# Sums over partitions moved from GpSimd to TensorE, and the first block's unfold copied inside SBUF

## The chip, the cores and the metric

The kernel runs on one core of one Trainium2 chip. The metric is device time in microseconds (us) for one execution, as the median of several runs. A smaller number is better. The page and the trace come from one profiled execution, which has its own time and its own span.

The engines are called as in the trace: PE is TensorE, DVE is VectorE, ACT is ScalarE, POOL is GpSimd, SP is SyncE, which here only issues transfers. SPq, ACTq, DVEq and POOLq are the sequencers of these engines, and PEld is the loading of weights into PE.

## What is computed

The input is x of 16 batches, each 128 rows by 1024 columns, with a context of the same shape. The block does two gated steps:

```
xn  = layernorm(x)
sim = cosine similarity of each ctx column with its left neighbour, itself, its right neighbour
att_out[o,t] = sum over (c,k) of weight[o,c,k] * xn[c, t+k-1] * sim[k,t]     (K = 3)
x1  = x + tanh(g_xattn) * att_out

h   = relu(layernorm(x1) @ up_w) ** 2            (1024 -> 2048)
s   = h @ down_w                                  (2048 -> 1024)
r   = ((layernorm(x1) @ fc1_w) @ expert_w) * routing_sum @ fc2_w
out = x1 + tanh(g_ffn) * layernorm(s + r)
```

The routing sum of a row is the sum of the two largest of eight logits, layernorm(x1) @ gate_w.

The unfold is the step that matters here: the 128 x 3 = 384 rows (channel c, shift k) of shifted xn, in the order 3c + k, are laid over three groups of 128 partitions, so that PE can contract over them. Row r of the unfolded matrix is channel r // 3, shifted by r % 3.

Matmuls of the steady part run on pairs of float16 numbers, a high and a low part. Each weight is first scaled by a power of two. The exponent comes from a sum or a maximum over the whole weight, so it needs a reduction over the 128 partitions. There are five such scales besides up_w's: the two small weights w_xattn and w_gate (WX, WG, computed together), fc1 (WF1), the product expert x fc2 (W2E) and down_w (WDN).

## The kernel before, in words

The 16 batches are taken in NB = 4 blocks of BB = 4 batches, j = 0 to 3. For each block there is an attention step (called phase a), then `up_half` (20 tiles t of the latent and hidden layer, 24 matmuls each), then `down_half` (for each batch 96 matmuls of `shared` and 24 of `routed`). The attention step of block m + 1 is woven into `up_half(m)` and `down_half(m)`. The attention step of block 0 has nothing to be woven into: it stands alone at the front with the loading, scaling and splitting of all weights. This front is where the change lies.

Each engine runs its own written list of instructions in order. The engines meet at semaphores. Nothing is reordered at run time, so what stands behind a waiting instruction on an engine waits too. SP's list issues nearly all loads and stores, and holds a wait wherever a transfer needs a buffer or data.

Names, in the order of the front:

- ACT's `first_f_pairs(j)` normalises batch j and writes the high part (semaphore f_hi). POOL subtracts to make the low part (line 575, f_rdy). ACT's batch j >= 2 waits until POOL is done with batch j - 2. The pair lies in `fp[j]`.
- DVE takes the maxima of each partition of the two small weights into `amx` (amax_rdy 1). POOL reduces these over the partitions with `partition_all_reduce` (line 579), which stands in POOL's list between the low part of batch 0 and that of batch 1 (amax_all 1). The same is done for fc1 (line 582), for W2E (line 601) and for down_w (line 607, inside `up_half(0)`).
- ACT's square root at line 848 stands behind all four `first_f_pairs`. DVE's `first_cosines` needs it (line 999 on), and only then can SP store the similarities and load them back, spread over 128 partitions (`first_sims(j)`, lines 338 and 339).
- SP's `first_unfold(j)` waits for f_rdy, writes the pair three times to DRAM with shifts of 0, 1 and 2 columns (line 322, 512 KB each), waits for these to land, and reads the unfolded rows back in one transfer of 1.5 MB (line 333) into `U[j % 2]` (u_buf for even j, a part of lgb for odd j).
- SP's order behind that is: unfold(0), load of fc1, store of the similarities, sims(0), unfold(1), sims(1), unfold(2), sims(2), three loads of up_w (line 481), unfold(3), sims(3), five more loads of up_w. unfold(2) and unfold(3) wait for PE to have used the buffer (p_done).
- PE's `xattn(0, j, h)` (line 1363) uses `U`, for each half h of the columns. DVE's `combine(0, j)` (lines 1043 to 1059) applies the similarities and adds, ACT's line 677 normalises, PE turns (line 1384).
- ACT's `up_squares(k)` (line 814) squares a 1 MB slice of up_w when it has landed, and PE sums the squares by columns (line 1522). They stand between the batches' steps in ACT's list. After them come DVE's scale of up_w (line 1293 and behind), W2E's scale, and the splitting of 16 tiles of up_w (ACT line 769, DVE line 1163), with which `up_half(0)` begins.

## Time and profile before

| what | us |
|---|---|
| median of 3 runs | 1131.89 |
| lowest and highest of them | 1130.33, 1138.74 |
| the profiled execution: its time | 1136.75 |
| the profiled execution: its span | 1135.0 |
| PE busy in the span | 1005.7 (89%) |
| DVE busy | 553.9 (49%) |
| ACT busy | 301.0 (27%) |
| POOL busy | 256.0 (23%) |
| moved by transfers | 175.31 MB |

The busy share of an engine is an average over the whole span. The page's second part cuts the span in 40 slices of 28.4 us: PE shows 5, 5, 8, 5, 6 tenths in the first five, the front, and 9 nearly everywhere from slice 13 on. The transfer engines show 8, 4, 9, 8, 7 tenths in the first five and 2 to 5 tenths for most of the rest.

In a row of the timeline the first number is the start from the span's start, the second the time from there to the end of the last of the group. What stands in square brackets is how long the engine had been idle, and what ended it. "issue" there means that the engine waited for nothing that the profile shows.

### The profile page before, as it was taken

How to read it: one execution, taken by the hardware profiler on the slowest of the kernel's cores; microseconds unless marked ns; L12 is line 12 of the kernel's file. 1: busy time of each engine (PE TensorE's matmuls, PEld its weight loads, DVE VectorE, ACT ScalarE, POOL GpSimd, SP SyncE). 2: the span in 40 equal slices, each digit the busy share in tenths (PEclk: the TensorE clock that was granted, in tenths of full speed). 3: DMA queues.
4: the chain of work that ended last, by engine and by line, in shares of the span. 5: the costliest groups of instructions: out<-in, count | busy, mean ns of one | idle time of the engine just before them, and what ended most of it. 6: DMA issues, size and time to landing. Idle time of an engine off the chain costs nothing.

```text
span 1135.0 us, 13061 instructions
## 1 busy us (share of the span) xinstructions
PE 1005.7 (89%) x4773; PEld 466.4 (41%) x4775; DVE 553.9 (49%) x987; ACT 301.0 (27%) x413; POOL 256.0 (23%) x170
## 2 busy tenths in 40 slices
PE   5585699486779999999899999997999999999996
PEld 4232243132334444444344444443444444444442
DVE  3367677457674552666354553674455522221112
ACT  4335554564311111223011121232011112220110
POOL 4211112227452223222022113330022220000121
PEclk9698699787889999999899999999999999999998
DMA  8498788843533323374433325556233323310000
GB/s 296 165 308 325 289 296 292 322 179 111 188 129 130 129 94 133 115 263 173 137 130 111 112 94 187 202 201 226 93 130 104 105 89 107 99 38 1 19 19 38
DMA packets 55587, 175.31 MB, mean 154 GB/s; under 512 B 6818, under 2 KB 7010, under 8 KB 54498
## 3 DMA queue, kind: packets, MB, share of 16 engines
q1 hardware_dynamic: 50050, 155.05, 39.0%
q10 hardware_dynamic: 5472, 19.40, 4.5%
q8 instruction: 40, 0.66, 0.3%
q14 instruction: 25, 0.20, 0.1%
HBM read 130.26 MB, written 44.17 MB: 154 GB/s over the span
## 4 chain that ended last, share of the span: by engine, by line
PE 61%; DMA 11%; DVE 8%; issue 8%; POOL 3%; ACT 3%; DVEq 2%; SPq 1%; POOLq 1%; ACTq 1%
PE psS L1426 27%; PE psS L1399 12%; PE psR L1399 10%; PE psR L1437 7%; PE psP L1363 5%; DMA shift_scratch<-hid 4%; DMA work<-in_x 2%; DMA u_buf<-shift_scratch 1%; DMA scr<-in_ctx 1%; DMA pair_scratch<-hid 1%; POOL f_pair L521 1%; POOLq L503 1%; DMA big<-in_L_ffn_up_w 1%; DMA shift_scratch<-f_pair 1%; DVE hid L1163 1%
## 5 line engine op out<-in xcount | busy, mean ns | idle before, releaser
L1426 PE MATMUL psS<-big,hid 128*128 128x512 f16 x1536 | 346.3, 385 | 7.9 <-ACT y L699 7.9
L1399 PE MATMUL psS<-xT,ring 128*128 128x512 f16 x960 | 216.3, 386 | 18.7 <-DMA ring<-pair_scratch 14.8
L1426 PEld LDWEIGHTS psS<-big,hid 128*128 128x128 f16 x1536 | 151.5, 99 | 192.3 <-issue 10.0
L1399 PE MATMUL psR<-xT,ring 128*128 128x512 f16 x960 | 214.2, 383 | 9.6 <-DMA ring<-pair_scratch 8.2
L1399 PEld LDWEIGHTS psS<-xT,ring 128*128 128x128 f16 x960 | 94.8, 99 | 136.6 <-DMA ring<-pair_scratch 15.2
L1399 PEld LDWEIGHTS psR<-xT,ring 128*128 128x128 f16 x960 | 94.0, 98 | 126.7 <-issue 10.2
L513 POOL TENSOR_TENSOR y<-y,lgb 128x1024 f32<-128x1024 f32 x15 | 35.2, 2346 | 490.6 <-ACT y L691 490.6
L647 ACT ACTIVATE sd<-sd 128x1 f32<-128x1 f32 x44 | 8.9, 202 | 374.5 <-DVE sd L917 374.5
L1437 PE MATMUL psR<-w,lgb 128*128 128x512 f16 x384 | 86.0, 379 | 0.0
L1363 PE MATMUL psP<-u_buf,wx 128*128 128x512 f16 x252 | 62.8, 397 | 11.3 <-DMA u_buf<-shift_scratch 8.8
L1200 DVE TENSOR_TENSOR hid<-sim_side,hid 128x512 f16<-128x512 f32 x64 | 53.1, 829 | 34.9 <-ACT hid L726 32.9
L1125 DVE SCALAR_TENSOR_TENSOR y<-psR,rw,y 128x1024 f32<-128x1024 f32 x15 | 19.2, 1282 | 102.3 <-PE psR L1437 99.9
L1043 DVE SCALAR_TENSOR_TENSOR scr<-psP,coef,sim_side 128x512 f32<-128x512 f32 x28 | 20.9, 748 | 97.0 <-PE psP L1363 89.9
L726 ACT ACTIVATE hid<-sim_side 128x512 f16<-128x512 f32 x64 | 40.3, 630 | 95.9 <-DVEq L1194 95.9
L1437 PEld LDWEIGHTS psR<-w,lgb 128*128 128x128 f16 x384 | 37.5, 98 | 44.7
L501 POOL TENSOR_TENSOR sides<-scr 128x1023 f32<-128x1023 f32 x12 | 22.7, 1890 | 121.3 <-DMA scr<-in_ctx 104.3
L1191 DVE SCALAR_TENSOR_TENSOR sim_side<-psS,sim_side 128x512 f32<-128x512 f32 x32 | 22.1, 690 | 50.6 <-ACT sim_side L724 49.8
L908 DVE BATCH_NORM_STATS2 st<-work 128x6 f32<-128x512 f32 x52 | 34.8, 688 | 19.1 <-DMA work<-in_x 16.9
L1363 PEld LDWEIGHTS psP<-u_buf,wx 128*128 128x128 f16 x252 | 24.9, 101 | 45.5 <-issue 16.4
L1191 DVE SCALAR_TENSOR_TENSOR sim_side<-psR,sim_side 128x512 f32<-128x512 f32 x32 | 22.0, 689 | 40.0 <-ACT sim_side L724 38.8
L521 POOL TENSOR_TENSOR f_pair<-work,f_pair 128x1024 f16<-128x1024 f32 x12 | 26.0, 2164 | 56.5 <-ACT f_pair L671 56.5
L1106 DVE TENSOR_TENSOR xT<-psP,xT 128x512 f16<-128x512 f32 x25 | 16.1, 686 | 41.5 <-ACT xT L684 41.5
(225 smaller groups left out, 1002.4 us busy)
## 6 DMA issues: line engine op xcount, KB each, us to landing
ring<-pair_scratch SPq DMA_DIRECT2D x80, 512.0 KB, 5.8
u_buf<-shift_scratch SPq DMA_DIRECT2D x14, 1536.0 KB, 6.4
shift_scratch<-f_pair SPq DMA_DIRECT2D x39, 512.0 KB, 3.8
work<-in_x SPq DMA_DIRECT2D x26, 512.0 KB, 5.8
big<-in_L_ffn_up_w SPq DMA_DIRECT2D x8, 1024.0 KB, 14.1
pair_scratch<-hid ACTq DMA_DIRECT2D x16, 512.0 KB, 5.6
out_rows<-y SPq DMA_DIRECT2D x15, 512.0 KB, 2.6
sim_side<-side_scratch SPq DMA_DIRECT2D x14, 512.5 KB, 4.1
```

The lines of the kernel that those rows point to most:

```text
L501: pool.tensor_tensor(sides_a[:, 0:T - 1], scr[0][:, 0:T - 1], scr[0][:, 1:T], ALU.mult)
L513: pool.tensor_tensor(y[:, :], y[:, :], gam, ALU.mult)
L521: pool.tensor_tensor(fp[0][:, 1, 1:T + 1], work[:, 0, :], fp[0][:, 0, 1:T + 1], ALU.subtract)\
L726: act.activation(hT[:, t - LT, 0, :], buf, ACT.Copy).then_inc(h_hi, 1)
L908: dve.bn_stats(st[:, k, h, :], src[:, HALF * h:HALF * h + HALF])
L1043: dve.scalar_tensor_tensor(out=left, in0=psP[:, 0, :], scalar=c_x, in1=sim_side[b][:, t0:t0 + HALF], op0=ALU.mult, op1=ALU.mult)
L1191: dve.scalar_tensor_tensor(out=hbuf[:, t % 2, :], in0=bank, scalar=0.0, in1=hbuf[:, t % 2, :], op0=ALU.max, op1=ALU.mult)
L1200: dve.tensor_tensor(hT[:, t - LT, 1, :], hbuf[:, t % 2, :], hT[:, t - LT, 0, :], ALU.subtract).then_inc(h_rdy, 1)
L1363: mm = pe.matmul(psP[:, g, :], wx[:, g, w, :], U[b][:, g, v, t0:t0 + HALF], start=(n == 0), stop=(n == 2))
L1399: mm = pe.matmul(up_bank[t % NR], ring[:, t % NR, a, k, :], xT[:, k, b, :], start=(k == 0 and a == 0 and b == 0), stop=(k == KB - 1 and a ...
L1426: mm = pe.matmul(psS[:, HALF * h:HALF * h + HALF], hT[:, i, a, P * j:P * j + P], dn[:, i, b, HALF * h:HALF * h + HALF], start=(i == 0 and ...
L1437: mm = pe.matmul(psR[:, HALF * h:HALF * h + HALF], lat[:, l, a, P * j:P * j + P], w2[:, l, b, HALF * h:HALF * h + HALF], start=(l == 0 and ...
```

## The change

Five edits belong together.

1. The four `partition_all_reduce` of POOL are taken out. In their place PE multiplies a 128 x 128 matrix of ones (`ones_f`, one more memset on POOL) with the one or two columns of `amx`, so that each partition of a PSUM column holds the sum (`norm_over_rows`). DVE copies that column into `amr` before it computes the power of two. For WX and WG the maximum over partitions becomes a sum of the partitions' maxima.
2. These matmuls have fixed places in PE's list: WX and WG behind `first_sums`; WF1 between `xattn(0, 0, 0)` and `expert_fc2(1)`; W2E ahead of `up_half(0)`; WDN behind tile t = 12 of `up_half(0)`. Each waits for `amax_rdy`.
3. `first_unfold(j)` no longer goes through DRAM. It copies from `fp[j]` to `U[j % 2]` inside SBUF. For each of the three groups and three shifts one transfer of 42 rows (168 KB, to every third partition) is issued, and for six of the nine one more transfer of a single row: 15 transfers for a batch, 60 for the block, where there had been four, 16 for the block. There is no wait between them any more.
4. Counts of semaphores that follow from it: `u_in` counts 15 transfers for a batch of the first block, `shift_out` starts from zero with block 1, and ACT's `f_pairs` of the first batch of block 1 does not wait for it.
5. `combine(0, j)` on DVE first waits for f_rdy of a batch two ahead (it overwrites the buffer `scr` that POOL reads), and ACT drains behind the square of fc1.

```diff
+    ROWS = P // G
+    UIN_0 = 16 * (G * G + P * G - ROWS * G * G)
...
+        norm_at = {WX: psP[:, 2, 8:10], WF1: psM[:, 500:501], W2E: psP[:, 2, 0:1], WDN: psP[:, 2, 1:2]}
...
@@ SP, first_unfold(j)
                 sp.wait_ge(f_rdy, j + 1)
                 sp.wait_ge(pads_rdy, 1)
                 if j >= 2:
-                    sp.wait_ge(u_in[j % 2], UIN * (j // 2))
-                shifts_out(j, j)
-                sp.wait_ge(shift_out, 16 * G * (j + 1))
-                if j >= 2:
                     sp.wait_ge(p_done, 2 * (j - 1))
                 if j == 1:
                     sp.wait_ge(eT_done, LT)
-                unfold_into(j, j % 2)
+                for g in range(G):
+                    for k in range(G):
+                        p0 = (k - P * g) % G
+                        c0 = (P * g + p0) // G
+                        num = (P - p0 + G - 1) // G
+                        p1 = p0 + G * ROWS
+                        sp.dma_start(U[j % 2][p0:p1 - G + 1:G, g, :, :],
+                                     fp[j][c0:c0 + ROWS, :, k:k + T]).then_inc(u_in[j % 2], 16)
+                        if num > ROWS:
+                            sp.dma_start(U[j % 2][p1:p1 + 1, g, :, :],
+                                         fp[j][c0 + ROWS:c0 + ROWS + 1, :, k:k + T]).then_inc(u_in[j % 2], 16)
@@ POOL
+            pool.memset(ones_f[:, :], 1.0)
...
-                if j == 0:
-                    pool.wait_ge(amax_rdy, 1)
-                    pool.partition_all_reduce(amr[:, WX:WG + 1], amx[:, WX:WG + 1], P, RMAX)\
-                        .then_inc(amax_all, 1)
-            pool.wait_ge(amax_rdy, 2)
-            pool.partition_all_reduce(amr[:, WF1:WF1 + 1], amx[:, WF1:WF1 + 1], P, RADD).then_inc(amax_all, 1)
...
-            pool.wait_ge(amax_rdy, 3)
-            pool.partition_all_reduce(amr[:, W2E:W2E + 1], amx[:, W2E:W2E + 1], P, RADD).then_inc(amax_all, 1)
...
-                    if first and j == BB - 1:
-                        pool.wait_ge(amax_rdy, 4)
-                        pool.partition_all_reduce(amr[:, WDN:WDN + 1], amx[:, WDN:WDN + 1], P, RADD)\
-                            .then_inc(amax_all, 1)
@@ DVE, combine and norm_scale
                 if first:
+                    dve.wait_ge(f_rdy, min(j + 3, BB))
                     dve.wait_ge(sim_in[b], 32 * (j // 2 + 1))
...
                 dve.wait_ge(amax_all, turn)
+                dve.tensor_copy(amr[:, k:k + 1], norm_at[k])
+                dve.drain()
@@ PE
+            def norm_over_rows(k, n, turn):
+
+                pe.wait_ge(amax_rdy, turn)
+                pe.matmul(norm_at[k], ones_f[:, :], amx[:, k:k + n], start=True, stop=True,
+                          skip_group_check=True).then_inc(amax_all, 1)
...
                     mm.then_inc(up_done, 1)
+                    if first and t == SCALE_T:
+                        norm_over_rows(WDN, 1, 4)
...
             pe.drain().then_inc(sums_done, 1)
+            norm_over_rows(WX, 2, 1)
...
             xattn(0, 0, 0)
+            norm_over_rows(WF1, 1, 2)
             expert_fc2(1)
...
             pe.wait_ge(norms_read, 1)
-            up_half(0, True)
+            pe.wait_ge(comb, 2 * BB)
+            norm_over_rows(W2E, 1, 3)
+            up_half(0, True, True)
```

SP's list before, from the unfold of batch 0 to the reading back of batch 1 (f_pair and hid hold the pairs, u_buf and lgb the unfolded rows):

```order
L322 DMA shift_scratch<-f_pair 128x2x1024 [waits pads_rdy,f_rdy]
L322 DMA shift_scratch<-f_pair 128x2x1024 x2
L333 DMA u_buf<-shift_scratch 128x3x2048 [waits shift_out]
L468 DMA big<-in_L_ffn_fc_w 128x8x512
L314 DMA side_scratch<-hid 32x128 [waits simo_rdy]
```

The same stretch of SP's list now:

```order
L383 DMA u_buf<-f_pair 42x2x1024 [waits pads_rdy,f_rdy]
L386 DMA u_buf<-f_pair 1x2x1024
L383 DMA u_buf<-f_pair 42x2x1024
L386 DMA u_buf<-f_pair 1x2x1024
L383 DMA u_buf<-f_pair 42x2x1024 x2
L386 DMA u_buf<-f_pair 1x2x1024
...
L477 DMA big<-in_L_ffn_fc_w 128x8x512
L317 DMA side_scratch<-hid 32x128 [waits simo_rdy]
```

The wait on shift_out is gone from between the two halves of the unfold, and 15 issues stand where four stood.

PE's list now, in `up_half(0)` around tile t = 12; the fourth row is new, the others stood there before in this order:

```order
L1409 MATMUL psR<-xT,ring 128x512 x23
L1409 MATMUL psS<-xT,ring 128x512 [waits up_evac,ring_in0]
L1409 MATMUL psS<-xT,ring 128x512 x23
L1329 MATMUL psP<-amx,ones_f 128x1 [waits amax_rdy]
L1409 MATMUL psS<-xT,ring 128x512 [waits up_evac,ring_in1]
L1409 MATMUL psS<-xT,ring 128x512 x23
```

Tile 13 and all behind it now stand behind a wait for amax_rdy, which on PE there was not.

## Rows read from the trace of the kernel before

**Rows 1.** Busy us by stage; columns: stretch, length, engines, PEclk, DMA share, GB/s
```profile
0.00:142.30 142.30, 88.00 (x347) 47.30 (x349) 77.36 (x140) 61.44 (x67) 35.70 (x52) 0.83 0.77 277
142.30:295.50 153.20, 115.93 (x548) 51.34 (x549) 100.67 (x135) 79.45 (x109) 50.15 (x32) 0.87 0.65 235
...
668.00:910.00 242.00, 231.72 (x1134) 106.71 (x1133) 126.08 (x239) 49.96 (x78) 52.31 (x28) 0.99 0.43 148
```

**Rows 2.** Chain of waits in the front: start us, us, what
```profile
68.39 17.28 DMA shift_scratch<-hid
...
89.60 17.50 DMA shift_scratch<-hid
...
108.53 11.02 DMA big<-in_L_ffn_up_w
```

**Rows 3.** Timeline of POOL, 20 to 66 us: start, us, instruction, idle before
```profile
30.74 0.37 POOL L579 PARTITION_ALL_REDUCE amr<-amx  x1 [5.83 <-issue]
40.82 2.13 POOL L575 TENSOR_TENSOR hid<-hid 128x1024 f16<-128x1024 f32 x1 [9.71 <-issue]
```

**Rows 4.** Timelines of ACT, DVE and PE, 40 to 66 us
```profile
43.06 1.24 ACT L660 ACTIVATE hid<-hid,rs_x 128x1024 f32<-128x1024 f32 x1 [13.81 <-POOL hid L575]
45.66 2.06 DVE L999 TENSOR_SCALAR hid<-hid 32x129 f32<-32x129 f32 x1 [12.47 <-ACT hid L848]
47.59 9.80 PE L1510 MATMUL psS<-big,home 128*128 128x512 f32 x16 [11.25 <-ACT home L852]
61.96 0.75 DVE L1043 SCALAR_TENSOR_TENSOR scr<-psP,coef,sim_side 128x512 f32<-128x512 f32 x1 [7.07 <-DMA ring<-self_scratch]
```

**Rows 5.** Timeline of SP: issues of the unfold and of up_w
```profile
24.94 2.67 SPq L322 DMA_DIRECT2D shift_scratch<-f_pair  x3
31.18 0.36 SPq L333 DMA_DIRECT2D u_buf<-shift_scratch  x1
...
87.10 1.41 SPq L481 DMA_DIRECT2D big<-in_L_ffn_up_w  x3
...
108.53 2.48 SPq L481 DMA_DIRECT2D big<-in_L_ffn_up_w  x5
```

**Rows 6.** Timelines of ACT and PE, 72 to 125 us
```profile
82.02 4.02 PE L1363 MATMUL psP<-lgb,wx 128*128 128x512 f16 x9
83.80 1.02 ACT L821 ACTIVATE w<-psS 128x1024 f32<-128x1024 f32 x1 [2.83 <-DMA pair_scratch<-xT]
113.47 4.02 PE L1363 MATMUL psP<-lgb,wx 128*128 128x512 f16 x9 [9.17 <-DMA lgb<-shift_scratch]
119.58 1.91 ACT L814 ACTIVATE sides<-big 128x2048 bf16<-128x2048 f32 x1 [11.34 <-DMA big<-in_L_ffn_up_w]
```

**Rows 7.** Timelines of POOL and DVE where W2E's scale is made
```profile
145.26 0.40 POOL L601 PARTITION_ALL_REDUCE amr<-amx  x1 [5.88 <-issue]
145.69 0.15 DVE L1111 TENSOR_SCALAR amr<-amr 128x1 f32<-128x1 f32 x1 [3.50 <-POOL amr L601]
```

**Rows 8.** Timelines of four engines where down_w's scale is made
```profile
242.34 0.40 POOL L607 PARTITION_ALL_REDUCE amr<-amx  x1 [6.46 <-DVEq L1169]
252.59 1.88 POOL L501 TENSOR_TENSOR sides<-scr 128x1023 f32<-128x1023 f32 x1 [9.84 <-issue]
251.51 0.57 ACT L724 ACTIVATE sim_side<-psS 128x512 f32<-128x512 f32 x1
254.59 1.25 DVE L951 STREAM_TRANSPOSE y<-sides 128x1024 f32<-128x1024 f32 x1 [1.79 <-POOLq L503]
245.05 8.26 PE L1399 MATMUL psR<-xT,ring 128*128 128x512 f16 x24 [3.75 <-DMA ring<-pair_scratch]
```

**Rows 9.** Rates and small instructions: transfers at 86 to 108 us, matmul, copy
```profile
86.00:108.00 22.00, 14.99 (x54) 7.02 (x54) 19.51 (x31) 14.13 (x17) 5.08 (x4) 0.97 0.89 334
...
268.88 0.57 PE L1327 MATMUL psM<-fold,part 128*128 128x1 f32 x2
...
299.72 0.18 DVE L1136 COPY lg<-psM 128x32 f32<-128x32 f32 x1
```

More of the change, by code:

```diff
@@ L25 @@
 I32 = mybir.dt.int32
-RMAX = bass.bass_isa.ReduceOp.max
-RADD = bass.bass_isa.ReduceOp.add
 P = 128
@@ L138, in flamingo_block @@
         ones_b = sb("ones_b", [P, P], BF16)
+        ones_f = sb("ones_f", [P, P], F32)
         pick = sb("pick", [P, 2 * BB * KB - 1], F32)
@@ L341, in first_unfolded @@
             def first_unfolded(m):
-                sp.wait_ge(shift_out, ahead(16 * G * BB * (m + 1)))
+                sp.wait_ge(shift_out, ahead(16 * G * BB * m))
                 unfold_into(0, 0)
@@ L667, in f_pairs @@
                 act.wait_ge(rs_rdy[LX], q + 1)
-                act.wait_ge(shift_out, 16 * G * q)
+                if not (isinstance(q, int) and q == BB):
+                    act.wait_ge(shift_out, 16 * G * (q - BB))
                 act.activation(work[:, 0, :], work[:, 0, :], ACT.Identity, bias=rs[:, LX, 1:2], scale=rs[:, LX, 0:1])
@@ L812, in up_squares @@
                 elif n == 1:
-                    act.wait_ge(u_in[0], UIN)
+                    act.wait_ge(u_in[0], UIN_0)
                 act.activation(squares[n % 2], up_raw[:, k, :], ACT.Square).then_inc(sq_rdy, 1)
@@ L860, in _ @@
             act.wait_ge(f1_in, 16)
-            act.activation(fc1_junk, fc1_raw, ACT.Square, accum_out=amx[:, WF1:WF1 + 1]).then_inc(amax_rdy, 1)
+            act.activation(fc1_junk, fc1_raw, ACT.Square, accum_out=amx[:, WF1:WF1 + 1])
+            act.drain().then_inc(amax_rdy, 1)
             w2_evac(0)
@@ L892, in _ @@
             for b in range(2):
-                act.wait_ge(u_in[b], 2 * UIN)
+                act.wait_ge(u_in[b], 2 * UIN_0)
             act.wait_ge(home_rdy, BB)
@@ L1271, in _ @@
             dve.wait_ge(amax_all, 1)
+            dve.tensor_copy(amr[:, WX:WG + 1], norm_at[WX])
+            dve.drain()
             pow2(WX, WG + 1, amr[:, WX:WG + 1], 2.0 ** -23, 0.0)
@@ L1285, in _ @@
                 .then_inc(gate_w_rdy, 1)
-            dve.wait_ge(amax_all, 2)
-            pow2(WF1, WF1 + 1, amr[:, WF1:WF1 + 1], 2.0 ** -24, 63.5)
+            norm_scale(WF1, 2)
             dve.drain().then_inc(scale_rdy, 1)
@@ L1350, in xattn @@
                 elif first:
-                    pe.wait_ge(u_in[b], UIN * (j // 2 + 1))
+                    pe.wait_ge(u_in[b], UIN_0 * (j // 2 + 1))
                     if j == 0:
@@ L1357, in xattn @@
                 else:
-                    pe.wait_ge(u_in[0], UIN * (q - 1))
+                    pe.wait_ge(u_in[0], 2 * UIN_0 + UIN * (q - BB + 1))
                     pe.wait_ge(xt_rdy, 2 * q)
@@ L1386, in turn_first, with up_half @@
                 mm.then_inc(tr_done, 1)
-            def up_half(n, phase_a):
+            def up_half(n, phase_a, first=False):
                 m = n + 1
```

## The prediction, made before the changed kernel had run

> **What bounds the kernel now.** I read the busy time by stage first, then the chain of waits, then the timelines of the front. The stages [rows 1] show that PE works 231.72 of 242.00 us in an ordinary block: there it is the bound, and the change touches nothing there. In the front it works 88.00 of 142.30 us, and in the first `up_half` 115.93 of 153.20. From the first `down_half` on the program is the same instructions in the same order, so what the front loses or gains should reach the end one to one. The question is only when the front's last results are there.
>
> Two things stretch the front. The first is POOL. It finished the low part of batch 0 at 24.9, and then stood 5.83 us before the first all-reduce ran and 9.71 us behind it before it could make the low part of batch 1 [rows 3]. ACT waited 13.81 us for that low part, and with it the square root that stands behind; DVE waited 12.47 us for the square root, and PE 11.25 us for ACT's copies of the expert weights behind the same list [rows 4]. The second is SP's queue. The chain of waits runs through the landing of the shifted copies in DRAM, 17.28 us for batch 2 and 17.50 us for batch 3, and only then are the last five loads of up_w issued, at 108.53; the first of these lands 11.02 us later [rows 2]. ACT had been idle 11.34 us for it, and PE 9.17 us for the unfolded rows of batch 3 [rows 6]. The transfers were busy 77% of the front at 277 GB/s [rows 1], which is much, but not all.
>
> **The change, part by part.**
>
> POOL without the first all-reduce. ACT was free at 43.06 - 13.81 = 29.2 and had made the high parts of batches 1 and 2 just before, 2.3 us each, so that of batch 1 was ready about 27, before the first all-reduce had begun to run. Its low part then takes 2.13 us [rows 3] and ends at 29, when ACT is just free. So ACT's 13.81 us go entirely. DVE's square root comes then at about 32.4 instead of 45.6; DVE itself reaches line 999 about a microsecond sooner too, since WX's result comes from a small matmul as soon as `first_sums` has ended. What stays of the 12.47 us is under half a microsecond. PE's 11.25 us go the same way. The three inputs of the first `combine` (PE's product, the similarities, and their transfer, for which DVE waited 7.07 us until 61.96 [rows 4]) all hang on this one root and move together: I take **13.0 us**, with ends at 12.0 and 13.8. The all-reduce of WF1 had other work beside it (PE's fc2 product) and is costed at nothing; if that cover went, 6 us would show, but the product is 9.80 us long [rows 4].
>
> Here a page bears on the size. The trace shows a gap of 5.83, 5.88 and 6.46 us ahead of three all-reduces and of 9.71 and 9.84 us behind two of them [rows 3, 7, 8]. The Trainium skill, GPSIMD Engine Reference, section "Instruction dispatch", states about 6 us for the first call to a freshly loaded kernel; of the way back to ordinary instructions it says nothing. By the page alone this term would be near 6 us instead of 13. The trace has the gap behind as well, both times.
>
> The middle of the front. The wait of ACT for the stored fc1 pairs, 2.83 us [rows 6], stood behind 1.5 MB of shifted copies in the same queue; a queue with half that traffic should shorten it. Ends 0 and 2.83; **2 us**.
>
> The unfold inside SBUF. For each batch three writes, a wait and one read become 15 copies. The issue of a transfer costs SP 0.89 us by the three at 24.94, 0.47 by the three at 87.10 and 0.50 by the five at 108.53 [rows 5]; the first row holds the one that the engine had just been waiting for, so I take 0.47, and 15 copies cost 7 us, at most 13. Nothing else of SP's is late by that: up to batch 1, the load of fc1 goes out behind the 15 copies at about 24.9 + 7 = 32, where it was 31.6. For batches 2 and 3 the wait for the landing is gone and the wait for PE's use of the buffer remains. For batch 3 that is the second half of batch 1, which ended at 86.0 [rows 6]. Moved by 13 + 2 it ends at 71; 7 us of copies and 1 us for the similarities bring the five loads of up_w to 79, where they were at 108.53. With the same 11.02 us to land [rows 2] the first is there at 90. ACT was ready for it at 119.58 - 11.34 = 108.2, which becomes 93. So the wait falls to nothing with 3 us to spare. PE's 9.17 us lie beside ACT's and are no term of their own.
>
> The bytes speak the same: each batch now moves 1.5 MB instead of 3. From the unfold of batch 1 on, about 14 MB have to pass before ACT's slice is there (three unfolds 4.7, three pairs of similarities 3.1, stored fc1 2.1, four slices of up_w 4.2), and at the 334 GB/s of a loaded stretch [rows 9] that is 42 us, from 43, when the first of them is issued, to 85. So the gain is the full 11.34 if the copies run at the rate of other transfers, and nothing if they run so slowly that they bring the old wait back. I take **10 us**; ends 0 and 11.34.
>
> W2E. DVE waited 3.50 us for the all-reduce [rows 7]. In its place stand a matmul of one column, about 0.3 us (two took 0.57 [rows 9]), a copy of 0.18 [rows 9] and a drain: 0.8 in all with the semaphores. **2.7 us**; ends 2.0 and 3.2.
>
> WDN. DVE reached its result late, and it was not waited for. But POOL, 9.84 us behind it, came late with the products that DVE waited 1.79 us for [rows 8]; that can come back. Against it, PE now waits behind tile 12 for amax_rdy, which DVE posted just before POOL's 242.34 [rows 8]. Tile 13 starts then at 242.5 instead of right behind tile 12. With the granted clock down after such a pause a tile of 24 takes up to 8.26 us [rows 8], so tile 13 is there by 250.8; ACT took it at 251.51 [rows 8]. The cover is thus 0.7 us at its thinnest: PE was two tiles ahead of ACT there, its tile 15 ended at 253.3 [rows 8], and this lead is what gets used up. Ends -3 and +1.79; I take **0**.
>
> The new copies on DVE, ACT's drain and the memset are 0.2 us each; they are in the terms above or beside idle time. DVE's added wait for f_rdy of a batch two ahead is met at about 34, before the first `combine`.
>
> Sum: 13.0 + 2 + 10 + 2.7 + 0 = 27.7 us. The profiled execution took 1136.75, so 1109.0 by it. The median of the runs shown is 1131.89, which is 4.9 lower, so the forecast is **1104 us**.
>
> **The rivals.**
>
> The copies bring the wait for up_w back. Copies with 42 rows and an odd shift could run well below the 334 GB/s, and the transfers are the fullest resource of the front. Then the third term is lost: 27.7 - 11 gives 17, or 1115. For it: 77% busy already. 
>
> Slower: the copies are served one after another, each with its own fixed time d. Three unfolds lie on the front's path, 45 copies. The forecast has 21 us in them and 3 to spare; all 27.7 are eaten when 45 d = 21 + 3 + 27.7, so d = 1.15 us. At 1.3 us it is 7 us slower, 1139. Against it: three shifted copies of 512 KB were issued in 2.67 us and had all landed by 31.18 [rows 5], 2.1 us a piece with three times the bytes, and 172 KB at 334 GB/s are 0.5 us. The same page, section "Rules for kernel authors", calls transfers under 64 KB mostly overhead and counsels to merge them. By its fixed 2 us for a transfer, taken one after another, the copies would make the kernel 1170. Chance 5%, and 8% for the stretch between, within 1% of before.
>
> **How the numbers follow.** The forecast holds 61%, with its own range 1097 to 1111: ends of the terms add to about 33 at best, and the two ends of 0 and -3 seldom come together. The range 1096 to 1118 takes in most of the first rival too. A measurement of this kernel can tell about 1% from no change, 11.3 us, so faster is below 1120.6. That is the forecast, the second rival and nearly all of the first: 0.87. Within 1%: 0.08. Slower: 0.05.
>
> **What would show each step.** POOL's low part of batch 1 starts near 27 and ACT's idle before line 660's last row is gone. DVE reaches the first `combine` near 49. SP issues 15 copies in about 7 us and the last five loads of up_w near 79. ACT doesn't wait for up_w, and DVE's scale of up_w comes some 25 us sooner. W2E costs DVE under 1 us. PE has a gap of 12 us behind tile 12 without a later tile of ACT moving. From then on every row is 28 us earlier. It is wrong if SP is seen issuing a copy in over 1 us, or if the unfolded rows land over 10 us behind the last issue.

## The result, and the profile after

The changed kernel took 1118.38 us (median of 4 runs, 1116.14 to 1118.85) beside 1131.71 us for the kernel before on the same chip (4 runs). The ratio is 0.9861, with a 95% interval of 0.9833 to 0.9889. The forecast was 1104 us, with a range of 1096 to 1118. The sign was right. The size was about half to two thirds of what was forecast: as it stands the median lies 0.4 us above the range, and by its ratio, on the 1131.89 us that the forecast started from, it is 1116.2, just inside. The profiled execution took 1118.56 us, with a span of 1116.7, which is 18.3 us shorter than the one before (1135.0), where 27.7 were forecast. The medians are only 13.3 us apart, since the profiled execution of the kernel before (1136.75 us) was itself 5 us above its median. The steps below are differences of these two executions; a repeat (experiment 5) gave 19.4 us between medians.

The stages come first. Columns: stretch, length, busy us of PE, PEld, DVE, ACT and POOL, granted clock, DMA share, GB/s.

```profile
0.00:142.30 142.30, 98.90 (x405) 51.38 (x408) 86.56 (x157) 68.51 (x73) 40.10 (x54) 0.89 0.76 258
142.30:295.50 153.20, 122.94 (x581) 55.05 (x580) 98.61 (x139) 79.94 (x109) 55.57 (x33) 0.88 0.64 232
668.00:910.00 242.00, 231.80 (x1135) 106.88 (x1134) 126.14 (x239) 50.24 (x77) 52.04 (x29) 0.99 0.41 147
```

Against [rows 1], an ordinary block is the same (231.80 us of PE beside 231.72), and the two front stages hold 10.9 and 7.0 us more of PE's work: work has moved forward. The first matmul of the first `down_half` tells how far (timeline of PE, the kernel before and then the changed one; columns: start us, us, instruction).

```profile
295.55 14.67 PE L1426 MATMUL psS<-big,hid 128*128 128x512 f16 x60
```

```profile
276.82 14.89 PE L1438 MATMUL psS<-big,hid 128*128 128x512 f16 x60
```

It is 18.7 us earlier, and that accounts for the gain of the span (18.3). The rest of this section follows it back.

**The start of the front.** Timelines of POOL, DVE and PE of the changed kernel. The bracket is the idle time ahead of an instruction and what ended it.

```profile
27.02 2.15 POOL L585 TENSOR_TENSOR hid<-hid 128x1024 f16<-128x1024 f32 x1 [2.15 <-ACT hid L660]
33.52 0.44 DVE L999 TENSOR_SCALAR hid<-hid 32x129 f32<-32x129 f32 x1 [0.40 <-ACT hid L847]
35.67 7.13 PE L1523 MATMUL psS<-big,home 128*128 128x512 f32 x16 [0.84 <-ACT home L851]
49.90 0.59 PE L1329 MATMUL psM<-amx,ones_f 128*128 128x1 f32 x2 [5.15 <-ACTq L861]
52.19 0.75 DVE L1044 SCALAR_TENSOR_TENSOR scr<-psP,coef,sim_side 128x512 f32<-128x512 f32 x1 [0.76 <-DMA ring<-self_scratch]
```

POOL's low part of batch 1 starts at 27.02 where it started at 40.82 [rows 3], and of the four waits of 12.47, 11.25, 13.81 and 9.71 us [rows 3, 4] less than 1 us is left on any engine, besides POOL's 2.15 us for ACT. DVE is at line 999 at 33.52 instead of 45.66, 12.1 us earlier. But its first `combine` is at 52.19 instead of 61.96 [rows 4], only 9.8 earlier. Two arrivals that stand ahead of it were late, and within a microsecond of each other. One is WF1's scale, which DVE computes just ahead of `combine`: PE waited 5.15 us before the one-column sum for it. The other came last, by 0.76 us: the similarities, read back from DRAM. SP's timeline of the changed kernel, and then of the kernel before, where the store had gone out at 53.09:

```profile
39.34 0.36 SPq L317 DMA_DIRECT2D side_scratch<-hid  x1
46.47 0.36 SPq L341 DMA_DIRECT2D sim_side<-side_scratch  x1
```

```profile
54.98 0.36 SPq L338 DMA_DIRECT2D sim_side<-side_scratch  x1
```

The store was 13.75 us earlier, but the load that has to wait for it to land came 7.1 us behind it, where it had been 1.9. It went out just after fc1 had landed (46.11, below). Both late arrivals thus lead to the load of fc1.

**SP's queue.** Timeline of SP, with the 42-row copies (L383) and single rows (L386) of batches 0 and 2, and the loads behind them. "x3" joins three issues.

```profile
24.90 1.04 SPq L383 DMA_DIRECT2D u_buf<-f_pair  x1
...
36.48 0.63 SPq L386 DMA_DIRECT2D u_buf<-f_pair  x1
37.16 0.40 SPq L477 DMA_DIRECT2D big<-in_L_ffn_fc_w  x1
...
61.89 0.88 SPq L383 DMA_DIRECT2D u_buf<-hid  x1
...
68.91 1.78 SPq L386 DMA_DIRECT2D u_buf<-hid  x1
...
76.74 0.63 SPq L386 DMA_DIRECT2D u_buf<-hid  x1
...
78.76 1.66 SPq L490 DMA_DIRECT2D big<-in_L_ffn_up_w  x3
80.54 0.88 SPq L383 DMA_DIRECT2D lgb<-hid  x1
...
94.53 0.63 SPq L386 DMA_DIRECT2D lgb<-hid  x1
```

And the same issues by line; columns: instructions, then shortest, median and longest ns of one.

```profile
L383 SPq DMA_DIRECT2D u_buf<-f_pair x9: 807/852/1043, 24.9 to 35.6; - x9
L386 SPq DMA_DIRECT2D u_buf<-f_pair x6: 616/635/649, 26.0 to 36.5; - x6
L383 SPq DMA_DIRECT2D u_buf<-hid x9: 807/871/2237, 61.9 to 75.8; - x9
```

A 42-row copy costs SP 0.85 us and a single row 0.64, where 0.47 was assumed. The 15 of batch 0 take 37.11 - 24.90 = 12.2 us and those of batch 1 take 12.0; those of batches 2 and 3 take 15.5 and 14.6, as some single issues stretch to 1.8 and more there, with the transfers busy (0.88 from 60 to 96 us, shown with the seventh experiment). From 61.89 until the last five loads of up_w go out, SP issues almost without a pause.

**The end of the front.** Timelines of ACT, PE and DVE, changed kernel.

```profile
46.11 3.62 ACT L860 ACTIVATE home<-big 128x4096 bf16<-128x4096 f32 x1 [9.79 <-DMA big<-in_L_ffn_fc_w]
73.23 1.02 ACT L820 ACTIVATE w<-psS 128x1024 f32<-128x1024 f32 x1 [1.98 <-DMA pair_scratch<-xT]
97.95 4.02 PE L1373 MATMUL psP<-lgb,wx 128*128 128x512 f16 x9 [5.21 <-DMA lgb<-hid]
105.65 1.91 ACT L813 ACTIVATE sides<-big 128x2048 bf16<-128x2048 f32 x1 [8.98 <-DMA big<-in_L_ffn_up_w]
129.03 0.16 DVE L1175 COPY amr<-psP 128x1 f32<-128x1 f32 x1 [0.77 <-PE psP L1329]
129.28 0.15 DVE L1112 TENSOR_SCALAR amr<-amr 128x1 f32<-128x1 f32 x1
223.23 0.59 PE L1329 MATMUL psP<-amx,ones_f 128*128 128x1 f32 x2 [11.28 <-DVEq L1170]
```

SP issues the last five loads of up_w at 96.53 (shown with the third experiment), and ACT's wait for them is still 8.98 us, where it was 11.34 [rows 6]. ACT is there at 105.65 instead of 119.58, 13.9 earlier. The first instruction of W2E's scale, at 129.28 behind the new copy, is 16.4 earlier than the same one at 145.69 [rows 7], so 2.5 came from its all-reduce. PE's stand of 11.28 us behind tile 12 was foreseen. The start of `down_half` is 2.3 us further ahead than W2E was, so no cost of the stand shows here; the eighth experiment prices it.

### The profile page after: what moved, and what is told of

Same layout as the page of the kernel before. It is cut to its first block, busy times and chain, and to the rows that moved or that the text cites. A ratio compares the mean times of both kernels' runs of the same rounds, so it can differ in the third digit from the quotient of the medians.

```text
span 1116.7 us, 13108 instructions
## 1 busy us (share of the span) xinstructions
PE 1004.0 (90%) x4781; PEld 466.2 (42%) x4783; DVE 550.6 (49%) x991; ACT 301.2 (27%) x413; POOL 256.2 (23%) x167
## 4 chain that ended last, share of the span: by engine, by line
PE 64%; issue 9%; DMA 7%; DVE 7%; SPq 4%; POOL 3%; ACT 3%; DVEq 2%; POOLq 1%; ACTq 0%
PE psS L1438 28%; PE psS L1409 12%; PE psR L1409 10%; PE psR L1449 7%; PE psP L1373 5%; SPq L383 2%; DMA pair_scratch<-hid 2%; DMA u_buf<-shift_scratch 1%; SPq L386 1%; POOL f_pair L530 1%; DMA scr<-in_ctx 1%; DMA shift_scratch<-f_pair 1%; POOL scr L513 1%; PE psR L1523 1%; DMA big<-in_L_ffn_up_w 1%
## 5 line engine op out<-in xcount | busy, mean ns | idle before, releaser
L1409 PE MATMUL psS<-xT,ring 128*128 128x512 f16 x960 | 221.1, 392 | 12.5 <-DMA ring<-pair_scratch 10.9
L1409 PE MATMUL psR<-xT,ring 128*128 128x512 f16 x960 | 210.8, 379 | 3.7 <-DMA ring<-pair_scratch 3.7
L1409 PEld LDWEIGHTS psS<-xT,ring 128*128 128x128 f16 x960 | 96.4, 101 | 133.2 <-issue 15.4
L1126 DVE SCALAR_TENSOR_TENSOR y<-psR,rw,y 128x1024 f32<-128x1024 f32 x15 | 19.2, 1282 | 102.3 <-PE psR L1449 99.8
L1203 DVE TENSOR_TENSOR hid<-sim_side,hid 128x512 f16<-128x512 f32 x64 | 49.3, 770 | 34.9 <-ACT hid L725 32.9
L725 ACT ACTIVATE hid<-sim_side 128x512 f16<-128x512 f32 x64 | 40.3, 630 | 94.5 <-DVEq L1197 94.5
```

Of the source, the lines that this page charges most:

```text
L725: act.activation(hT[:, t - LT, 0, :], buf, ACT.Copy).then_inc(h_hi, 1)
L1203: dve.tensor_tensor(hT[:, t - LT, 1, :], hbuf[:, t % 2, :], hT[:, t - LT, 0, :], ALU.subtract).then_inc(h_rdy, 1)
L1409: mm = pe.matmul(up_bank[t % NR], ring[:, t % NR, a, k, :], xT[:, k, b, :], start=(k == 0 and a == 0 and b == 0), stop=(k == KB - 1 and a ...
```

## The experiments

The question was where the rest had gone. **Theory S**: SP's time for the issues. 15 copies hold its queue for 12 us or more, so that the load of fc1 and those of up_w go out late. **Theory T**: the transfer engines are nearly full, and the loads of up_w would land late whenever they were issued. The names behind the headings are those that the expectations use. The before-kernel's median was 1135.68 us beside the first four experiments, 1137.43 beside the next four and 1133.58 beside the last two; ratios go by these.

**1. The sums on TensorE alone.** (e1_sums_only) The unfold goes through DRAM as before.

```diff
-                for g in range(G):
-                    for k in range(G):
...
+                shifts_out(j, j)
+                sp.wait_ge(shift_out, 16 * G * (j + 1))
...
+                unfold_into(j, j % 2)
```

> The sums and maxima are on PE as in the changed kernel, the first block's unfold goes through DRAM as before. Theory S (SP's issue time: in the changed kernel a 42-row copy took SP 0.85 us and a single row 0.64 us, 12.2 us for the 15 of a batch, so the unfold inside SBUF gave away most of what it saved): the POOL stall is the main gain, 12.5 to 13 us at the first combine, plus 2.7 at W2E and up to 2 at WDN, and the old unfold keeps its waits; 1113 to 1118 us, level with the changed kernel or a few us better. Rival T (the transfers' bytes bound the front, and the unfold inside SBUF with half of them is a gain of its own): 1121 to 1125, slower than the changed kernel by 3 us or more.

Measured: 1121.5 us, ratio 0.9881 (0.9858 to 0.9903), so 14 us of gain (11 to 16). DVE, SP's queue and ACT, in the profile of this kernel:

```profile
51.34 0.75 DVE L1037 SCALAR_TENSOR_TENSOR scr<-psP,coef,sim_side 128x512 f32<-128x512 f32 x1 [2.04 <-DMA ring<-self_scratch]
98.38 2.52 SPq L484 DMA_DIRECT2D big<-in_L_ffn_up_w  x5
109.59 1.91 ACT L806 ACTIVATE sides<-big 128x2048 bf16<-128x2048 f32 x1 [11.51 <-DMA big<-in_L_ffn_up_w]
```

ACT's wait for up_w is as long as before (11.51 us), and it ends 10.0 us earlier than the 119.58 of [rows 6]. Most of the whole change's gain is this part. The loads of up_w leave only 1.9 us later than with the copies, although the unfolds of four batches through DRAM stand ahead of them. `down_half` begins at 280.15, 3.3 us later than in the changed kernel: that is what the unfold inside SBUF adds to the sums, against the 10 us forecast for it. The theories are not told apart. On the 1132 us of the expectations, S had meant a gain of 14 to 19 us and T one of 7 to 11, so the gain is at S's lower end and above T's; but T's "3 us or more" behind the changed kernel is what the two traces show, while the intervals of the two ratios overlap.

**2. The unfold inside SBUF alone.** (e2_unfold_only) POOL keeps its all-reduces.

```diff
+                if j == 0:
+                    pool.wait_ge(amax_rdy, 1)
+                    pool.partition_all_reduce(amr[:, WX:WG + 1], amx[:, WX:WG + 1], P, RMAX)\
+                        .then_inc(amax_all, 1)
...
```

> The unfold runs inside SBUF as in the changed kernel, the four reductions stay on POOL. Theory S: POOL's stall hides nothing of the 12 us that SP now needs for each batch, but the waits for landings are gone too; the last five loads of up_w are issued near 99 us instead of 108.5, ACT's wait for them is shorter, and the kernel gains 2 to 8 us on the one before: 1124 to 1130. If all gains were additive as in the prediction it would gain 10 to 12: 1120 to 1122. Rival T: with half the bytes ACT waits no longer for up_w at all: 1120.

Measured: 1126.83 us, ratio 0.9921 (0.9899 to 0.9943), 9 us of gain (6.5 to 11.5). By its median that is just above the 2 to 8 of theory S and below the 10 to 12 of additive gains. The timeline of POOL:

```profile
30.85 0.37 POOL L587 PARTITION_ALL_REDUCE amr<-amx  x1 [5.95 <-issue]
38.10 2.13 POOL L583 TENSOR_TENSOR hid<-hid 128x1024 f16<-128x1024 f32 x1 [6.88 <-issue]
```

POOL's stall is there with both gaps, so it belongs to the all-reduce; the second gap is 6.88 us here and was 9.71. 14 and 9 make 23, and the two together gave 16 to 18 (by 0.9861 here, by 0.9844 in the repeat below). The traces say it more sharply: `down_half` begins 15.4 us earlier with the sums alone, 9.2 with the unfold alone (286.39), and 18.7 with both. So the parts share a resource. That it is SP's queue, which the copies have made fuller, is the reading that experiments 3 and 6 test.

**3. The load of fc1 ahead of the first copies.** (e3_fc1_first) Nothing else is changed.

```diff
-            first_unfold(0)
             sp.dma_start(fc1_raw, w_fc1.rearrange("(k p) l -> p k l", p=P)).then_inc(f1_in, 16)
+            first_unfold(0)
```

> The changed kernel with one edit: SP issues the load of fc1 ahead of the 15 copies of batch 0 instead of behind them. In the changed kernel it went out at 37.2 and landed at 46.1, ACT squared it then, and PE waited 5.15 us for the WF1 sum in front of the second fc2 product. Theory S (SP's issue time shifts fc1, fc1 holds PE's list): the load goes out at 25, lands near 32, PE has no wait at WF1, and the first combine starts near 49 instead of 52.2: 3 us better, 1115. Rival (the first combine is held by the similarities' landing, not by the WF1 sum): under 1 us, 1118.

Measured: 1114.35 us, ratio 0.9808 (0.9783 to 0.9834); the interval overlaps that of the changed kernel's repeat (0.9823 to 0.9866) a little. PE, DVE, SP and ACT:

```profile
47.34 0.28 PE L1329 MATMUL psM<-amx,ones_f 128*128 128x1 f32 x2
48.84 0.75 DVE L1044 SCALAR_TENSOR_TENSOR scr<-psP,coef,sim_side 128x512 f32<-128x512 f32 x1 [0.27 <-issue]
41.23 0.37 SPq L341 DMA_DIRECT2D sim_side<-side_scratch  x1
92.31 3.91 SPq L490 DMA_DIRECT2D big<-in_L_ffn_up_w  x5
101.20 1.91 ACT L813 ACTIVATE sides<-big 128x2048 bf16<-128x2048 f32 x1 [8.71 <-DMA big<-in_L_ffn_up_w]
```

In the changed kernel these loads left later (timeline of SP):

```profile
96.53 3.43 SPq L490 DMA_DIRECT2D big<-in_L_ffn_up_w  x5
```

PE's 5.15 us are gone, the first `combine` is at 48.84 instead of 52.19, and the loads, ACT's scale and the end of the front (272.86 instead of 276.82) are all about 4 us earlier. One transfer behind 15 issues instead of ahead of them had cost 4 us: that agrees with theory S for this place. It does not decide against the rival in the expectation, that the similarities' landing holds `combine`: their load too went out 5.2 us earlier, at 41.23 instead of 46.47, 1.9 us behind its store. Experiment 1 shows that this path would have held alone. There PE waited only 0.40 us for WF1, and yet `combine` stood 2.04 us for the similarities and began at 51.34, 0.85 earlier than in the changed kernel. Both paths had to be freed, and the one edit frees both.

**4. Six of the up_w loads ahead of batch 3's copies.** (e4_upw_early)

```diff
-                for k in (UP_ORDER[0:3], UP_ORDER[3:8])[j - 2]:
+                for k in (UP_ORDER[0:6], UP_ORDER[6:8])[j - 2]:
```

> The changed kernel with one edit: six of the eight loads of up_w are issued ahead of the unfold of batch 3 instead of three. In the changed kernel ACT waited 8.98 us for the fourth. Theory S (the fourth load was late because SP spent 14.7 us on issuing the copies of batch 3 ahead of it): ACT's wait goes, PE's wait for the unfolded rows of batch 3 (5.21 us) stays or grows by 1 to 2; 5 to 8 us better, 1110 to 1113. Rival T (the transfer engines were the limit, so what goes earlier delays the unfold by as much): within 2 us of the changed kernel, 1117 to 1120.

Measured: 1120.16 us, ratio 0.9862 (0.9837 to 0.9887): no gain. The timeline of PE:

```profile
106.48 4.02 PE L1373 MATMUL psP<-lgb,wx 128*128 128x512 f16 x9 [14.24 <-DMA lgb<-hid]
```

ACT no longer waited for up_w, but PE waited 14.24 us for batch 3's rows, instead of 5.21: their last copy was issued at 95.5 and PE could start only at 106.5, 11.0 us later, with 6 MB of weights issued ahead of these copies; in the changed kernel it was 94.5 and 97.95, 3.4 us. So the engines that move the bytes are a second limit. Reordering alone changed who is late, as theory T has it, and S's forecast for this run (1110 to 1113) was wrong.

**5. The changed kernel once more** (e0_after_again), with no edit, as the measure for the next three.

> The changed kernel again, beside the kernel before and the variants on one chip. The ratio to the kernel before should be 0.984 to 0.989. Theory S+T (SP's issue time and the full transfer queues together hold the front) and the prediction's own sum differ here only in that the sum of 27.7 us would give 0.976; the sum is excluded if the interval stays above 0.980.

Measured: 1118.06 us, ratio 0.9844 (0.9823 to 0.9866). The five loads leave at 96.40 and ACT's wait is 9.33 us until 105.50: the same picture. The interval lies above the 0.976 that the forecast's sum of 27.7 us would give.

**6. Each 42-row copy cut into 32 and 10 rows.** (e6_rows_32_and_10) The bytes are the same, with 24 issues for a batch instead of 15. If SP's issues are the limit, the time must grow with their number.

```diff
+                        pm = p0 + G * 32
-                        sp.dma_start(U[j % 2][p0:p1 - G + 1:G, g, :, :],
-                                     fp[j][c0:c0 + ROWS, :, k:k + T]).then_inc(u_in[j % 2], 16)
+                        sp.dma_start(U[j % 2][p0:pm - G + 1:G, g, :, :],
+                                     fp[j][c0:c0 + 32, :, k:k + T]).then_inc(u_in[j % 2], 16)
+                        sp.dma_start(U[j % 2][pm:p1 - G + 1:G, g, :, :],
+                                     fp[j][c0 + 32:c0 + ROWS, :, k:k + T]).then_inc(u_in[j % 2], 16)
```

> The changed kernel with each copy of 42 rows cut into one of 32 rows and one of 10. Question: why does a 42-row copy cost SP 0.85 us and a row 0.64 us, while a copy of 128 rows by 4 KB cost it 0.47? Theory K (SP pays extra where a copy does not spread evenly over the 16 queues: 42 rows and 1 row do not, 32 rows do): a 32-row copy costs 0.4 to 0.5 us, a 10-row copy 0.6 to 0.85. Rival N (the cost follows the number of rows, or the step of three partitions, or SBUF on both sides): a 32-row copy costs 0.75 to 0.8 us, a 10-row copy 0.65 to 0.7. With 24 copies for a batch the issue takes 12 to 14 us by K and 17 us by N; the kernel is 0 to 4 us slower by K, 8 to 14 us by N.

Measured: 1135.1 us, one run; the whole gain is gone. Timelines of SP, ACT and PE (L384 is the 32-row copy, L386 the 10-row one, L389 the single row):

```profile
27.39 0.65 SPq L384 DMA_DIRECT2D u_buf<-f_pair  x1
28.09 0.81 SPq L386 DMA_DIRECT2D u_buf<-f_pair  x1
28.93 0.63 SPq L389 DMA_DIRECT2D u_buf<-f_pair  x1
...
42.90 0.41 SPq L480 DMA_DIRECT2D big<-in_L_ffn_fc_w  x1
...
116.33 2.80 SPq L493 DMA_DIRECT2D big<-in_L_ffn_up_w  x5
124.54 1.91 ACT L816 ACTIVATE sides<-big 128x2048 bf16<-128x2048 f32 x1 [13.31 <-DMA big<-in_L_ffn_up_w]
296.01 15.01 PE L1441 MATMUL psS<-big,hid 128*128 128x512 f16 x60
```

Nine more issues of about 0.6 us are 5.4 us for a batch and 22 for four. fc1 goes out 5.7 us later, up_w 19.8 later, ACT's scale 18.9 later and `down_half` begins 19.2 later. The same bytes with more issues move the end nearly one to one: SP's queue is on the path through the whole front. Were the transfers the limit instead, they would be full; while SP issued without a gap from 74.8 to 116.3 us, they were busy 0.68 of the time (columns as for the stages):

```profile
75.00:116.00 41.00, 22.91 (x76) 10.38 (x76) 23.51 (x42) 17.23 (x20) 8.73 (x6) 0.83 0.68 205
```

This is the most direct evidence for S, though its time rests on one run. That the size of a copy sets its issue time is only partly so: 32 rows cost 0.64 us, 1 row 0.63, 10 rows 0.81, 42 rows 0.85. Neither theory of the expectation fits: K wanted 0.4 to 0.5 us for 32 rows, N 0.75 to 0.8, and both put the time 3 us or more too low.

**7. Through DRAM, but early.** (e7_dram_early) Sums on TensorE; every batch's shifted copies are written to DRAM well ahead of the read back, each with a semaphore of its own; fc1 goes first, and the loads of up_w are spread as 2, 2 and 4. SP's list becomes:

```diff
+            sp.dma_start(fc1_raw, w_fc1.rearrange("(k p) l -> p k l", p=P)).then_inc(f1_in, 16)
+            first_shifts(0)
+            first_unfold(0)
+            first_shifts(1)
+            store_first_sims()
+            first_sims(0)
+            first_shifts(2)
+            first_unfold(1)
...
+            first_shifts(3)
+            load_up(UP_ORDER[0:2])
+            first_unfold(2)
+            first_sims(2)
+            load_up(UP_ORDER[2:4])
+            first_unfold(3)
+            first_sims(3)
+            load_up(UP_ORDER[4:8])
```

> The sums stay on PE; the unfold goes through DRAM again, but the shifted copies of each batch are written early, two batches or more ahead of the reading, so that SP waits for no landing, and SP's issues for a batch fall from 15 to 4; fc1 is loaded first and the loads of up_w are spread. Theory S+T: with the issue time gone and the landings hidden, ACT's wait of 8.7 to 9 us for up_w goes and PE's wait for the unfolded rows of batch 3 shrinks; ratio 0.970 to 0.976 (1102 to 1108 where before is 1136), against 0.981 for the changed kernel with fc1 first. Rival T alone (the bytes bound the front; this variant moves 6 MB more): no better than the changed kernel, ratio 0.985 to 0.99.

Measured: 1113.12 us, ratio 0.9786 (0.9770 to 0.9802), below the repeat of the changed kernel (0.9823 to 0.9866) with twice its unfold's bytes; from experiment 3, which shares the early fc1, it can't be told. So neither forecast came (S and T together 0.970 to 0.976, T alone 0.985 to 0.99): the issues were worth something, and less than thought. ACT waits for up_w no more. The stretch from 60 to 96 us in this kernel, and then the same stretch in the changed one (columns as for the stages):

```profile
60.00:96.00 36.00, 27.84 (x93) 12.05 (x92) 31.74 (x49) 16.21 (x21) 7.85 (x7) 0.95 1.03 414
```

```profile
60.00:96.00 36.00, 27.88 (x100) 12.39 (x99) 30.47 (x50) 17.56 (x22) 10.00 (x7) 1.00 0.88 291
```

Here the transfer engines are full, at 414 GB/s. The changed kernel moved 291 with a share of 0.88: neither of its two limits was quite alone. A new wait stands where there was none, DVE's first `combine`:

```profile
54.28 0.75 DVE L1051 SCALAR_TENSOR_TENSOR scr<-psP,coef,sim_side 128x512 f32<-128x512 f32 x1 [7.38 <-DMA ring<-self_scratch]
```

**8. Experiment 3 with the sum of WDN two tiles later** (e8_wdn_later), to price PE's stand behind tile 12.

```diff
-                    if first and t == SCALE_T:
+                    if first and t == SCALE_T + 2:
                         norm_over_rows(WDN, 1, 4)
```

> The changed kernel with fc1 loaded first, and the sum for down_w placed behind tile 14 of the first up_half instead of tile 12, so that PE does not stand 11 us behind tile 12. Theory: the stand is hidden, since ACT takes the tiles later anyway; ratio within 0.1% of the variant with fc1 first, 0.980 to 0.982. Rival (the stand costs, as PE's lead is used up and the granted clock falls): 2 to 3 us better, 0.978 to 0.979.

Measured: 1113.33 us, ratio 0.9797 (0.9781 to 0.9813), inside experiment 3's interval. The sum's row in experiment 3, and here:

```profile
218.96 0.58 PE L1329 MATMUL psP<-amx,ones_f 128*128 128x1 f32 x2 [11.10 <-DVEq L1170]
```

```profile
218.94 0.28 PE L1329 MATMUL psP<-amx,ones_f 128*128 128x1 f32 x2
```

The stand of 11.10 us is gone and `down_half` begins at 272.23 instead of 272.86. Eleven idle microseconds of PE were worth about 0.6 in these two traces, and the times can't tell even that.

**9. Experiment 7 with the similarities' stores ahead of batch 1's shifted copies.** (e9_stores_first)

```diff
-            first_shifts(1)
             store_first_sims()
             first_sims(0)
+            first_shifts(1)
             first_shifts(2)
```

> The kernel of e7_dram_early (one-column sums on TensorE, the first unfold through DRAM with its shifted copies written early) in which the two stores of batch 0's similarities and their loads back stand ahead of the shifted copies of batch 1 on SP's queue, not behind them. In e7 the stores were issued at 39.26 us and the loads only at 47.45, and DVE's first combine waited 7.38 us for them until 54.28. Theory Q (a small store waits behind the large transfers issued ahead of it): the stores land within 3 us, the loads go out before 43 us, the first combine starts at or before 50 us, and the time falls by 3 to 5 us below e7's 1113.1, ratio to before about 0.975. Theory F (from 50 us on the transfer engines are full, and what comes early waits later): the first combine comes earlier, but U(1) and the up_w blocks come later by as much, and the time stays at 1112 to 1114, ratio 0.978 to 0.980.

**10. As 9, with batch 0 alone unfolded by the 15 copies in SBUF.** (e10_copies_for_batch_0)

```diff
-            first_shifts(0)
-            first_unfold(0)
+            copy_unfold(0)
...
```

> As e9_stores_first, but batch 0 alone is unfolded by the 15 copies from SBUF to SBUF, and batches 1 to 3 through DRAM. Theory S (SP's time for 15 issues is the price of the copies, where something waits behind them on its queue): batch 0's issue takes 12 us again, so the similarity stores leave at about 39 us where e9 has them earlier, and the time is 1 to 4 us above e9's. Theory D (what the copies save is the two trips through DRAM, and it is needed for batch 0 alone, before anything else is at hand): U(0) is there as early as in e9 or earlier, TensorE's first product starts no later than e9's, SP is free of 45 copies, and the time is at or up to 4 us below e9's.

Measured: experiment 9 1111.9 us, ratio 0.9802 (0.9773 to 0.9832); experiment 10 1110.45 us, ratio 0.9789 (0.9762 to 0.9816). The timelines of DVE and SP in experiment 9:

```profile
43.21 0.36 SPq L342 DMA_DIRECT2D sim_side<-side_scratch  x1
...
50.09 0.75 DVE L1051 SCALAR_TENSOR_TENSOR scr<-psP,coef,sim_side 128x512 f32<-128x512 f32 x1 [4.04 <-DMA ring<-self_scratch]
```

The first `combine` came 4.2 us earlier than in experiment 7, yet `down_half` began at 270.61 instead of 268.59. The time is F's (0.978 to 0.980) and not Q's (0.975): with the transfers full from 60 to 96 us (411 GB/s), what comes early waits later. In experiment 10 the stores of the similarities left at 39.36 us, where they left at 39.27 without the copies, so the 13 us of issues cost nothing there: SP had nothing else to do. S's forecast for this run was wrong, and it sharpens S: issue time costs only where something is queued behind it. D holds as far as the clock tells, but not in its detail: PE's first product starts at 45.45 us and not at 42.87, behind an fc2 product that took 9.29 us instead of 7.13. The intervals of experiments 3 and 7 to 10 overlap; they are not ranked here. Experiment 10 has the lowest median, 23 us under the kernel before, and its interval lies below that of the changed kernel (0.9833 to 0.9889), and just below that of the repeat (0.9823 to 0.9866).

## Why the prediction was partly right

**The first all-reduce (13.0 forecast).** Right at its source: POOL 13.8 us earlier, DVE's square root 12.1. At the first `combine` 9.8 were left. The step that failed is "move together": the prediction had all three inputs of `combine` hang on that one root, and held that "the load of fc1 goes out behind the 15 copies at about 24.9 + 7 = 32". It went out at 37.16 and made two things late. ACT's sum of it came late, and PE stood 5.15 us before WF1's matmul. The cost "at nothing" had a cover in fc2's product, but PE works through its list in order, and the new matmul puts a wait for fc1 on PE itself, ahead of that product. And the similarities' store was now followed by its load only 7.1 us later, where it had been 1.9. Experiment 3 moved only the load of fc1 and took back 4 us; how much of it each of the two paths held is not separated.

**The middle (2 forecast).** 0.85 came: the wait is 1.98 us instead of 2.83 [rows 6].

**The unfold (10 forecast).** This is the term that failed. From ACT's row at 73.23 (10.6 us earlier than in [rows 6]) to its row of up_w (13.9 earlier) only 3.3 us were won. Experiment 1 finds the same 3.3 from the other side. The step was the price of an issue: 0.47 us, "and 15 copies cost 7 us, at most 13". They cost 12.2, 12.0, 15.5 and 14.6. Even the 13 was written down and not carried through to what stands behind the copies. The prediction also let PE's use of the buffer set the start of batch 3's copies (71 us, and then 8 to the loads at 79). In fact batch 2's copies held SP until 77.4, three loads and batch 3's 15 issues followed, and the loads left at 96.5: 61.89 + 15.5 + 1.4 + 1.8 + 14.6 + 1.4, the 1.4 being the similarities and what lies around them. The queue itself had become the bound, and the two batches have to be added, not taken one at a time. Experiment 6 shows this causally. Behind it ACT still waited 8.98 us for the first of the five to land, where the prediction had the whole wait gone. The first rival named the right place (up_w's wait comes back, 1115 us), and not the right mechanism: it blamed the rate of the copies. The transfers' fullness was real, but a second limit (experiments 4, 7 and 9).

**The slower rival.** It had its break-even at 1.15 us for each copy of the three later batches. Measured were 12.0 to 15.5 us for 15, 0.80 to 1.03 each, as time on SP's queue and not as landings one after another. That was nearer to the break-even than a chance of 5% suggests, and with 24 issues for a batch (experiment 6) the kernel is indeed back at its old time.

**W2E (2.7 forecast).** Right: DVE's wait fell from 3.50 to 0.77 us, and with the copy in front its scale moved 2.5 us further ahead.

**WDN (0 forecast, -3 to +1.79).** Beyond the good end: 2.3 us won between W2E and `down_half` in all, and experiment 8 finds about 0.6 in the stand itself. What gave the 2.3, POOL's missing gap [rows 8] or something beside it, was not tried apart.

In sum: 9.8 + 0.85 + 3.3 + 2.5 + 2.3 = 18.7, instead of 27.7. These are successive stations of one pair of traces, so they must add up to the shift of `down_half`; the sum proves nothing by itself. The near hit of the range owes something to its width: the upper end had been put at 1118 to take in the first rival. Its own lower end of 1097 was also 2 us too low, since 1131.9 less the best ends of 33 is 1099.

## What to carry to other kernels

Count a queue's issues as work of an engine: multiply each shape's own issue time by its number, add batch to batch, and see what stands behind them in the same list; a cheap-looking row of another shape is no price. Before rewriting a burst of small issues, move a load that someone waits for ahead of it; here that one line was worth 4 us. When several inputs hang on one root, follow each of them to its arrival; what moves earlier can meet other traffic there. A wait that has its own engine to hide behind may lose the cover when it is moved to an engine that works in order, even if the operation itself takes 0.3 us. When two parts each gain alone, expect less from both if they feed the same queue.

## What the runs showed of the hardware

**Issue time on SP goes by shape.** From SBUF to SBUF, with 2,048-byte rows of two halves: 0.64 us for 32 rows, 0.63 for one, 0.81 for 10 and 0.85 for 42; 0.47 for a load of 128 rows from DRAM [rows 5]. When the transfers were loaded, a single small copy took up to 2.6 us (experiment 6), and in experiment 9, with them full, the issue of one batch's read took 5.14. The Trainium skill, DMA: Bandwidth & Descriptors, section "Why a DMA increments its semaphore by 16 and not by 1", says that a transfer on k engines, fewer than 16, leaves the issuing sequencer to write the other 16 - k increments itself. The 0.2 us that 10 and 42 rows cost more than 32 agree with that; the single row, which costs no more than 32, does not show it, and no run tried the number of engines apart from the number of rows.

**The gap behind an all-reduce on POOL** was 9.71 and 9.84 us before [rows 3, 8] and 6.88 in experiment 2, whose first unfold was the only thing different there. The gap ahead was 5.95 us, which agrees with the about 6 us that the Trainium skill, GPSIMD Engine Reference, section "Instruction dispatch", states for the first call to a freshly loaded kernel. Here it stood ahead of later all-reduces too (5.88 us before the third one, [rows 7]). Why the one behind varies stays open.

**A small store is late behind large transfers.** The similarities' two stores, issued at 39.3 and 39.7 us, were followed by their loads at 46.47 in the changed kernel (behind the load of fc1), at 47.45 in experiment 7 (behind 1.5 MB of shifted copies), at 43.21 in experiment 9 (behind the read of batch 0's rows), and at 41.23 in experiment 3 and 41.30 in experiment 10, with only the small copies in front.
